# Time mixing of a three-part transformer layer: rows asked for earlier, statistics and gate copies in another order, one low-rank product in column tiles

## The reference

```
xn  = layer_norm(x);  sx = previous token of xn - xn
xxx = tanh((xn + sx * maa_x) @ maa_w1)             # 5 low-rank products of 32 columns
x5  = xn + sx * (maa_stack + xxx[m] @ maa_w2[m])   # m = key, decay, value, receptance, gate
w   = exp(-exp(time_decay + tanh(x5[1] @ decay_w1) @ decay_w2))
r, k, v = x5[3] @ Wr.T, x5[0] @ Wk.T, x5[2] @ Wv.T;  g = silu(x5[4] @ Wg.T)
for each token:  out = r . (u * k v + s);  s = k v + w * s      # a 16 x 16 state in each of 32 heads
x   = x + (group_norm(out) * g) @ Wo.T
```

## Time and profile before

| | |
|---|---|
| median of 3 runs | 3070.8 us (3068.88 to 3071.51) |
| the profiled execution | 3071.39 us, its span 3069.6 us |
| TensorE, VectorE busy | 94%, 58% of the span |
| ScalarE, GpSimd busy | 38%, 17% of the span |
| granted TensorE clock, mean | 0.973 of full speed |
| time mixing | from 0 to about 751 us |
| scan multiplies, first to last (line 604) | 73.0 to 187.9, 255.0 to 369.6, 432.7 to 547.2, 604.6 to 719.4 us |

### The profile page before, as it was taken

How to read it: one execution, slowest core, us unless ns; L and a number is a source line. 1 busy time by engine, 2 the same in 40 slices (tenths; PEclk the granted TensorE clock), 3 DMA queues, 4 the chain that set the end, 5 groups by cost and what they waited for, 6 DMA issues and landing times.

```text
span 3069.6 us, 41094 instructions
## 1 busy us (share of the span) xinstructions
PE 2881.2 (94%) x14864; PEld 2179.8 (71%) x14864; DVE 1779.6 (58%) x2615; ACT 1163.7 (38%) x2537; POOL 534.8 (17%) x375
## 2 busy tenths in 40 slices
PE   5988889896897999999999999999999999999899
PEld 2333333332776888888888878888888888888787
DVE  5988979796866444455444464454444554444644
ACT  3232323221534343434434343354434453433432
POOL 2856747483001000001000010010000000000100
PEclk8989999997998999999999999999999999999999
DMA  5001010102124111110111112121110111111011
GB/s 159 1 13 43 1 56 0 42 0 73 67 80 159 55 38 55 38 55 32 38 55 38 55 35 62 41 90 38 55 38 31 55 39 55 38 49 33 22 55 55
DMA packets 54779, 148.71 MB, mean 48 GB/s; under 512 B 6256, under 2 KB 7536, under 8 KB 53584
## 3 DMA queue, kind: packets, MB, share of 16 engines
q1 hardware_dynamic: 51824, 143.80, 14.1%
q0 software_dynamic: 2880, 3.94, 0.6%
HBM read 131.20 MB, written 12.58 MB: 47 GB/s over the span
## 4 chain that ended last, share of the span: by engine, by line
PE 67%; DVE 2%; ACT 1%; issue 0%; DMA 0%; ACTq 0%; DVEq 0%
PE ca_ps L60 19%; PE ca_ps L62 19%; PE ca_ps L61 19%; PE ca_ps L1954 4%; PE ca_ps L1938 4%; PE ca_ps L1946 2%; PE ca_ps L1980 1%; DVE ca_stats L68 0%; DVE ca_xres L1715 0%; DVE ca_ctx_lo L1746 0%; DMA ca_xres<-in_ctxT 0%; DVE ca_wq_lo L1673 0%; ACT ca_sk L1631 0%; DVE ca_h_lo L1740 0%; ACT L1631 0%
## 5 line engine op out<-in xcount | busy, mean ns | idle before, releaser
L1715 DVE TENSOR_TENSOR ca_xres<-ca_xres,ca_ps 128x512 f32<-128x512 f32 x384 | 264.1, 688 | 243.8 <-PE ca_ps L62 238.9
L1502 ACT ACTIVATE ca_pr<-ca_ps,ca_nb 128x129 f32<-128x129 f32 x512 | 181.8, 368 | 511.0 <-DVE ca_nb L1698 510.9
L60 PE MATMUL ca_ps<-ca_h_hi,ca_wq_hi 128*128 128x512 f32 x768 | 312.7, 407 | 4.7 <-DVE ca_h_lo L1740 4.2
L609 DVE TENSOR_TENSOR_SCAN tm_xn<-tm_wd,tm_vb 128x512 f32<-128x512 f32 x256 | 298.5, 1208 | 12.0 <-POOL tm_xf L316 3.5
L62 PE MATMUL ca_ps<-ca_h_hi,ca_wq_lo 128*128 128x512 f32 x768 | 302.6, 394 | 0.0
L61 PE MATMUL ca_ps<-ca_h_lo,ca_wq_hi 128*128 128x512 f32 x768 | 300.6, 391 | 0.0
L60 PE MATMUL ca_ps<-ca_wv_hi,ca_ctx_hi 128*128 128x256 f32 x1024 | 298.0, 291 | 0.0
L62 PE MATMUL ca_ps<-ca_wv_hi,ca_ctx_lo 128*128 128x256 f32 x1024 | 287.6, 281 | 0.0
L61 PE MATMUL ca_ps<-ca_wv_lo,ca_ctx_hi 128*128 128x256 f32 x1024 | 287.3, 281 | 0.0
L1455 POOL TENSOR_TENSOR ca_dv<-ca_bvr 128x256 f32<-128x256 f32 x32 | 23.8, 745 | 1453.9 <-DVE ca_v L1683 1443.8
L60 PE MATMUL ca_ps<-ca_wo_hi,ca_ct_hi 128*128 128x512 f32 x640 | 253.5, 396 | 0.2 <-DVE ca_xres L1715 0.2
(11 more groups left out here) (232 smaller groups left out, 5799.6 us busy)
## 6 DMA issues: line engine op xcount, KB each, us to landing
ca_sq<-in_wq SPq DMA_DIRECT2D x49, 512.0 KB, 5.2
ca_so<-in_wo SPq DMA_DIRECT2D x48, 512.0 KB, 3.5
ca_sk<-in_wk SPq DMA_DIRECT2D x33, 512.0 KB, 6.5
ca_sv<-in_wv SPq DMA_DIRECT2D x32, 512.0 KB, 3.7
ca_bvr<-in_bvb SPq DMA_DIRECT2D x32, 256.0 KB, 3.9
tm_xq<-in_x SPq DMA_DIRECT2D x16, 256.0 KB, 4.5
tm_xres<-in_x SPq DMA_DIRECT2D x4, 1024.0 KB, 6.1
x_dram<-tm_xres SPq DMA_DIRECT2D x4, 1024.0 KB, 4.7
```

The source lines that it names most:

```text
L60: pe.matmul(out, lhs[0], rhs[0], start=first, stop=False)
L609: v.tensor_tensor_scan(state[t % 2][:, d, :], wd[:, g].rearrange("p b t -> p (b t)"), pair[:, d, :], 0.0, ALU.mult, ALU.add).then_inc(scan ...
L1502: ins = act.activation(pr[hd][:, b, :], ps[:, BANK_SC + b // 2, o:o + KW], ACT.Exp, bias=nbs[hd][:, b:b + 1], scale=SCALE, accum_out=sms[h ...
L1715: v.tensor_tensor(xres[U.h][:, U.quad * 4 + b, :], xres[U.h][:, U.quad * 4 + b, :], ps[:, BANK_O + b % 2, :], ALU.add).then_inc(o_out, 1)
```

## The change

- SyncE: the rows of quarter q+2 are requested in the stretch of quarter q, behind the residual's load and ahead of the store, and the next states with them. `quad` is gone, `load_rows` and `load_states` stand in its place, all written out.
- VectorE: the statistics of quarter q+2 are taken in `joint(q)`, two ahead of `gated(q, 2)`, two and the gathering behind `inverse(q, 3)`; only quarter 1's stay in `body(0)`. The wait for the last accumulation (`rs_used`) moves behind the small copy in `shift`. `mix(q+1, 1, 0)` goes ahead of `hidden_lo_last`. The loop is written out.
- ScalarE: `gate_mix(1)` comes ahead of `decay(2)` and `decay(3)`.
- TensorE: the fifth stack's low-rank product is four matmuls of 32 columns side by side, one per chunk, each into its own 32 partitions of bank `pj[0]`; ScalarE copies the bank out, and one matmul with the new constant `sum_parts` adds the four. `output(q, 1, 1)` comes earlier. The first value product waits for the fifth decay event, not the eighth.

```diff
-            def quad(q, first, last):
-                if not first:
+            def load_rows(q):
+                sp.wait_ge(xn0_ready, q * 4)
+                for b in range(4):
+                    load_x(q, b)
+
+            def load_states(q):
+                if q > 0:
                     sp.wait_ge(s0_set, q * STEPS)
                 sp.dma_start(s0[:], io["s0"][bass.ds(q, 1)].rearrange("a p c d b -> (a p) c d b")).then_inc(s0_in, 16)
...
+            for q in range(NQ):
                 sp.wait_ge(x2_out, q * 16 + 16)
                 sp.dma_start(xres[:], io["x"][bass.ds(q * 4, 4)].rearrange("b t e -> t b e")).then_inc(res_in, 16)
+                if q < NQ - 2:
+                    load_rows(q + 2)
+                if q < NQ - 1:
+                    load_states(q + 1)
                 sp.wait_ge(res_added, q * 4 + 4)
...
             def front(q, first):
...
+                act.wait_ge(lora_full, q * 4 + 2)
+                act.activation(ew[:], pj[0][:], ACT.Copy).then_inc(lora_out, 1)
+                act.wait_ge(lora_full, q * 4 + 3)
                 act.activation(h4, pj[0][0:LORA, :], ACT.Tanh).then_inc(lora_out, 1)
...
                 gate_mix(0)
+                gate_mix(1)
                 decay(2)
                 decay(3)
-                gate_mix(1)
...
             def shift(q):
                 v.tensor_copy(xn[:, :, :, 0], prev[:, :, bass.ds(q * 4, 4)]).then_inc(sx_ready, 1)
                 v.wait_ge(sx_ready, q * 5 + 1)
+                if q > 0:
+                    v.wait_ge(rs_used, q * STEPS)
...
             def joint(q):
+                more = q + 2 < NQ
+                if more:
+                    norm_stats(q + 2, 0)
+                    norm_stats(q + 2, 1)
                 gated(q, 2)
                 v.wait_ge(rs_ready, q * STEPS + STEPS)
-                v.wait_ge(rs_used, q * STEPS + STEPS)
                 shift(q + 1)
                 inverse(q, 3)
+                if more:
+                    norm_stats(q + 2, 2)
+                    norm_stats(q + 2, 3)
+                    norm_gather(q + 2)
                 hidden_lo(q + 1)
                 gated(q, 3)
+                mix(q + 1, 1, 0)
                 hidden_lo_last(q + 1)
...
-            with v.Fori(1, NQ - 1) as q:
+            for q in range(1, NQ - 1):
                 body(q, False)
                 joint(q)
...
+            def lora_last_parts():
+                for c in range(EC):
+                    ins = pe.matmul(pj[0][32 * c:32 * c + 32, :], lora1[:, c, P:P + LORA], xf[:, c, :], start=True, stop=True)
+                ins.then_inc(lora_full, 1)
+
+            def lora_last(q):
+                pe.wait_ge(lora_out, q * 4 + 2)
+                pe.matmul(pj[0][0:LORA, :], sum_parts[:], ew[:], start=True, stop=True).then_inc(lora_full, 1)
...
-                            pe.wait_ge(decay_out, q * 8 + 8)
+                            pe.wait_ge(decay_out, q * 8 + 5)
...
-                lora(n, 0, 3)
+                lora(n, 3)
+                pe.wait_ge(y_ready, q * 8 + 6)
+                lora_last_parts()
                 unpacks(q, 3)
-                pe.wait_ge(y_ready, q * 8 + 6)
-                lora(n, 1, 0)
-                lora(n, 1, 1)
                 first_output(q, 3)
-                lora(n, 1, 2)
-                lora(n, 1, 3)
                 output(q, 1, 0)
+                output(q, 1, 1)
+                lora_last(n)
```

More of the change, by code:

```diff
@@ L111, in time_mix @@
         pick_k = sb("pick_k", [P, 35])
+        sum_parts = sb("sum_parts", [P, LORA])
         spread_v = sb("spread_v", [P, 4, P])
@@ L589, in body @@
                     mix(q, 4, c, first)
-                    if not last:
+                    if first:
                         norm_stats(q + 1, c)
-                if not last:
+                if first:
                     norm_gather(q + 1)
@@ L908, in joint @@
                 mix(n, 1, 1)
-                output(q, 1, 1)
                 mix(n, 1, 2)
```

55 lines of the change are left out of this document (24 added, 31 removed).

## The result

The changed kernel takes 3054.9 us (median of five runs, 3048.9 to 3055.6) against 3068.9 (3065.9 to 3071.5) for the kernel before beside it: a ratio of 0.995, 95% interval 0.9938 to 0.9961. The time is inside the range forecast, 5.9 us above the forecast itself. The gain is 7.8 us short (14.0 where 21.8 were forecast): the changed kernel came out 5.9 higher, and the kernel before 1.9 lower than in the three runs that the forecast started from. The profiled execution took 3055.59, its span is 3053.8: 15.8 us shorter than that of before, where the sum said 22.15.

What follows compares the result with a forecast made beforehand. Time mixing was taken as bound by VectorE's scan steps within quarters and by waits between engines in the turns. Terms summed to 22.15 us off 3071.39, giving 3049.2, set at 3049.0; range 3043 to 3057.

Steps and rivals of the forecast that it cites:

- the sum: Time mixing's gains added: opening 3.4, turns 4.6 + 5.15, gate copies 6.3 + 0.6, low-rank and shift 2.1: 22.15 us.
- Part 1: Turns 0 and 1: early row requests and moved statistics save 4.98 and 5.63 us; scan waits of 1.81 and 1.73 go.
- rival (b): Moved statistics stand in the way in two turns, by late rows or short spare time: 3055.2 us; chance 0.10.
- Without them I take the clock to stay: Receptance product, turns 0 and 1: without statistics among the mixes TensorE keeps 2.4 GHz, saving 1.81 + 1.73 us.
- Part 2: VectorE's scan loop written out: quarters 1 and 2 lose 2.0 us each, 4.4 with last steps and scale operations.
- Rival (d): Writing VectorE's loop out costs nothing, the difference being something else: 3044.6 us; chance 0.07.
- Part 3: Earlier gate copy removes TensorE's hole (idle wait before the third gate-mix product): 2.1 us per turn, opening 3.4.
- Part 4: Last low-rank product in four column tiles, plus the shift's moved wait: 0.7 us per turn, opening 0.
- everything behind it should shift as a block: Stages behind the time mixing keep their length and only start earlier: 0 us gained or lost there.
- rival (a): Clock still falls in turns 0 and 1 and the opening; 3.5 and 1.3 us stay away: 3053.8 us; chance 0.24.
- Rival (e): Clock at 1.2 GHz through whole turns, a stretch of turn 1 alone costing up to 18 us: near 3085; chance 0.02.

Runs made afterwards that it cites:

- e1: The changed kernel run once more, nothing edited; median 3053.2 us.
- e7: The changed kernel with the next rows' statistics put back among the receptance mixes, rows still requested ahead; median 3053.1 us.
- e10: The changed kernel with statistics back among the receptance mixes and rows requested behind the residual's store again; median 3066.8 us.
- e5: The changed kernel with VectorE's quarters 1 and 2 as a real loop of two passes, statistics staying moved; median 3046.4 us.
- e6: The changed kernel, loop written out, with the scan's second wait put on the multiply ahead of it; median 3055.8 us.
- e2: The changed kernel with VectorE's body of every quarter set in a loop of one pass; median 3053.0 us.
- e9: The kernel before profiled once more, nothing edited; one run, last scan multiply at 717.12 us, 2350.4 us behind it.

## Why the prediction came out as it did

**Part 1, right in its size, partly wrong in its cause.** The last stretch of turns 0 and 1 is 8.21 us (8.25 forecast), the rows were there, and both third steps are short again. The statistics cost nothing where they went: in e1 the head of turn 0, with them, took 17.29 us and that of turn 2, without, 17.30. So rival (b) falls. But the step "Without them I take the clock to stay" named the statistics that spread the mixes out. e7 shows them spread out with the clock up, in both its turns; it took the wait for the rows, in before and in e10, to bring it down.

**Part 2, right.** 2.0 us each for quarters 1 and 2, and the cause by e5 and e6: two waits on the scan. Rival (d) falls. Not foreseen: one step of quarter 2 is 5.35 us instead of 5.0 in every profile with the written-out quarter 2 and its two waits on the scan except e2; why, stays open.

**Part 3, right, sized too low by 1.9 us in the turns.** The stretch with the hole gave 3.95, 2.44 and 2.42, where 2.7, 2.1 and 2.1 were taken. In turn 0 the lower clock behind the hole had cost 1.5, of which the forecast took 0.6; in e9 it cost nothing (6.34 us), so this 1.5 belongs to one execution and not to the kernel before. The opening gave 3.94 where 3.4 was taken, but over all profiles it takes 73.0 to 74.4 us with the hole and 68.8 to 71.4 without, so one pair can't tell these apart.

**Part 4, right, a little low.** 0.66 to 0.73 us a turn from the product and the order (0.5 forecast), and at equal clock 0.4 from the shift's wait, where 0.2 was taken: in turn 2 of before the small copy starts 7.78 us behind the last multiply and the first difference 0.30 behind the copy, in turn 2 of e1 it is 7.20 and 0.51.

**What failed: "everything behind it should shift as a block".** The sum has no term for the granted clock outside the stretches in which before and turn 2 differed. In the profiled execution the heads of turns 1 and 2 lost 3.8 us (turn 0 won 1.2), hidden in the total by what parts 3 and 4 gave beyond their terms, and 6.0 us were lost behind the last multiply, most of them with the lower clock. e1 shows that neither belongs to the change: the same program had two of its heads back at 17.3, and 5.6 of the 6.0 us. The profiles of e9 and e1 lie 19.7 us apart. Yet the medians, 3054.9 and 3053.2, lie above 3049.0, only 14.0 and 15.7 us below the kernel before beside them, and of the runs without a profile it can't be said where they lost it; that stays open. By the numbers this is near rival (a), 3053.8, but not by its mechanism: the clock did stay up in the stretches that (a) named, and fell in others. Rival (e) did not come up: the stretch that it priced, from the second decay mix to the third key mix, took 17.6 us in turn 1 as before. A small part of it did come up in other executions: in turns 0 and 2 of e1 the same stretch took 18.5 us, and in turn 0 the granted clock was 0.50 for 3 us of it (210.42 to 213.42).

One sum in the prediction is off as well: its own low bounds add up to 10.8 us and its high ones to 26.9, not to "some 12" and "some 29".

The Trainium skill, TensorE: Matmul & The Clock Gate, section HAM oscillation, says that pauses between bursts of matmuls bring the lower clock back. The profiles agree ahead of the heads: there the clock fell behind 0.77 us of work in 3. They also show that the same program at the same pauses gets its clock back some 3 us earlier in one execution than in the next, and that this decides between a head of 17.3 and one of 19.3 us or more.
